# Grouped attention and the norm behind it in one software-pipelined loop

## The chip, the cores and the metric

The kernel runs on one core of a Trainium2 chip. The metric is the device time of one execution in microseconds; of several executions the median is given. The engines are named as in the profile: PE is TensorE (PEld its weight loads), DVE is VectorE, ACT is ScalarE, POOL is GpSimd, SP is the engine that issues most DMAs. Each engine works through its own queue in order and waits on semaphores.

## The reference, cut to what matters

The program is a chain of blocks on a tensor of 16 images with 128 channels and 1024 tokens each, T = 16384 tokens in all. The change touches the last attention block and the norm behind it:

```python
t = t + L3_attn(_ln_t(t), ...)        # grouped attention
t = t + L3_ffn(_ln_t(t), ...)         # routing and experts

# in L3_attn, S = 1024, D = 128, G = 8 groups, H = 4 heads
q = (x @ Wq + bq).reshape(b, s, G, H, d)
k = (x @ Wk + bk).reshape(b, s, G, d)
v = (x @ Wv + bv).reshape(b, s, G, d)
scores = einsum('bqghd,bkgd->bqhg', q, k) / sqrt(d)   # k summed over all its tokens
weights = softmax(scores, axis=-1)                    # over the 8 groups
out = einsum('bqhg,bsgd->bsgd', weights, v).reshape(b, s, G * d)
return out @ Wo + bo

def _ln_t(v):                          # per token, over the 128 channels
    return (v - mean(v)) / sqrt(var(v) + 1e-5)
```

Since the scores use the sum of k over an image's tokens, and the weights enter only as their sum over an image's queries, an image costs little: 1024 x 32 scores from one matrix per image, a softmax over groups of 8, a sum of the weights over tokens and heads (8 numbers), and one 128 x 128 matrix A, the sum over the 8 groups of these numbers times a product of Wv and Wo.

## The kernel before, in words

The residual stream X (128 channels x 16384 tokens) stays in the on-chip memory for the whole program. Blocks follow one another, each with its own queues per engine and a barrier at its end. Three of them matter here; they take the stretch from about 4308 to 4587 us.

`phase_gqa` (from L2103) is grouped attention. It first makes what all images share (products of the weights, the score matrix and score bias of each image), then loops over 16 images b. For each: SP copies the image's normed tokens from Y to one of two buffers `ys` (L2148); PE writes the scores to the one bank `psc` (one product for the bias, L2178, and eight for the tokens, L2181); DVE takes the maximum of each 8 scores (L2251) and writes the differences to the one buffer `sc` (L2254); ACT takes the exponential in place (L2210); DVE sums, inverts and scales (L2260 to L2262, `weights`); PE sums the weights over tokens by a product with ones into the bank `pws` (L2188, `sums`); DVE reduces these to 8 numbers (L2268) and builds A with eight dependent multiply-adds (L2272, `mixing`); PE multiplies A with the image's Y (L2200, `outputs`, two banks `po`); DVE adds the result into X (L2280, `residual`).

The order in each engine's queue is written out by hand. In DVE's step for image b stand: maximum and subtract of b + 1, residual of b - 1, mixing of b, weights of b + 1. The subtract waits for the sums of b, because both use the one buffer `sc`. In PE's step for b stand: scores of b + 2 (after the subtract of b + 1 has emptied `psc`), outputs of b, sums of b + 1. `wait_if` (L383) is a semaphore wait that is left out in the first turns; `over` (L1031) peels the first and last turns of a loop; `Chain` makes each DVE instruction wait for the one before it.

`phase_norm` (L1816) with the tag n4 is the norm behind it, a block of its own over 32 chunks of 512 tokens with four buffers. For each chunk n, by the methods of `LayerNorm` (L1047): SP loads the chunk of X (L1069); PE transposes its four 128 x 128 tiles to token rows (L1076, front); DVE takes statistics (L1090, L1099); POOL makes scale and shift in four small instructions (L1108 to L1114); ACT normalizes (L1123) and issues the store of the token rows to the DRAM tensor `tokens` (L1841); PE transposes back (L1084); DVE copies the result to Y (L1129). Attention and this norm have separate tensors Y (`gqa_Y`, `moe_Y`).

`phase_route` follows, which reads Y, and then the experts, which read `tokens`.

Of the kernel before, what the change touches and what calls it, by code (L numbers as in the profile page):

```python
# [15 lines left out]
AX = mybir.AxisListType  # L16
# [1030 lines left out]
class LayerNorm:  # L1047
# [39 lines left out]
    def vector_stats(self, v, n, u):  # L1087
        v.wait_ge(self.front_ready, n + 1)
        for r in range(4):
            last = v.bn_stats(self.st[u][:, r, :], self.front[u][:, r, :])  # L1090
        last.then_inc(self.stat, 1)


        v.wait_ge(self.stat, 1)
        v.wait_ge(self.stat, n + 1)

        wait_if(v, self.ab_ready, n - self.r + 1)
        for r in range(4):
            last = v.bn_aggr(self.mv[u][:, r, :], self.st[u][:, r, :])  # L1099
        last.then_inc(self.mv_ready, 1)  # L1100
# [1002 lines left out]
def phase_gqa(nc, K, D, X, Y, W, w_in, sums):  # L2103
# [5 lines left out]
    with Mem(nc, "gq") as m:  # L2109
# [10 lines left out]
        sc = m.sb("sc", [C, TL, GH])  # L2120
# [4 lines left out]
        pa = m.ps("pa", [C, CH])  # L2125
        pc = m.ps("pc", [C, CH])
        pv = [m.ps(f"pv{h}", [C, 4, C]) for h in range(2)]
        psc = m.ps("psc", [C, TL, GH])
        pws = m.ps("pws", [C, TL, GH])
# [3 lines left out]
        sw_ready, sb_ready = m.sem("sw_ready"), m.sem("sb_ready")  # L2133
# [3 lines left out]
        NW = 3 + 1 + G8  # L2137
# [3 lines left out]

        with nc.Block() as block:
            @block.sync
            def _(sp):
                def step(b, u, last):
# [4 lines left out]
                over(sp, B, step)  # L2150

            @block.tensor
            def _(pe):
# [7 lines left out]
                last.then_inc(vo_mm, 1)  # L2161
                pe.wait_ge(ks_ready, 1)
# [5 lines left out]
                for g in range(G8):  # L2168
                    last = pe.matmul(pws[:, 0, g:g + 1], wo[:, g, :], bvT[:, g:g + 1], start=True, stop=True)
                last.then_inc(bvo_mm, 1)  # L2170
# [3 lines left out]
                def scores(b, u):  # L2174
                    pe.wait_ge(y_in[u], y_count(b, u))

                    wait_if(pe, sub_ready, b)
                    pe.matmul(psc[:, :, :], K["ident"][:, :], sb_[:, bass.ds(b, 1), :].to_broadcast([C, TL, GH]),  # L2178
                              start=True, stop=False)
                    for t in range(TL):  # L2180
                        last = pe.matmul(psc[:, t, :], ys[u][:, t * C:(t + 1) * C], sw[:, bass.ds(b, 1), :].rearrange("p o g -> p (o g)"),  # L2181
# [3 lines left out]
                def sums(b):  # L2185

                    pe.wait_ge(w_ready, b + 1)
                    pe.matmul(pws[:, :, :], K["ones"][:, :], sc[:, :, :], start=True, stop=True).then_inc(ws_mm, 1)  # L2188

                scores(0, 0)  # L2190
                sums(0)
                scores(1, 1)

                def step(b, u, last):
                    if not isinstance(b, int) or b + 2 < B:
                        scores(b + 2, u)
# [4 lines left out]
                    if not last:  # L2201
                        sums(b + 1)

                over(pe, B, step)

            @block.scalar
            def _(a):
                with a.Fori(0, B) as b:
                    a.wait_ge(sub_ready, b + 1)
                    a.activation(sc[:, :, :], sc[:, :, :], ACT.Exp, scale=C ** -0.5).then_inc(e_ready, 1)  # L2210

            @block.vector
            def _(v):
# [20 lines left out]

                for dst, src, mm, ready in ((sw, pa, sw_mm, sw_ready), (sb_, pc, sb_mm, sb_ready)):
# [5 lines left out]
                v.wait_ge(bvo_mm, 1)  # L2241
                step0(v.tensor_copy(vo[:, :, C], pws[:, 0, 0:G8]))

                scv = sc[:, :, :].rearrange("p t (h g) -> p (t h) g", g=G8)

                pscv = psc[:, :, :].rearrange("p t (h g) -> p (t h) g", g=G8)

                def below_max(b, st):

                    v.wait_ge(s_mm, b + 1)  # L2250
                    st(v.reduce_max(top[:, :], pscv, AX.X))  # L2251

                    wait_if(v, ws_mm, b)
                    v.tensor_tensor(scv, pscv, top[:, :].rearrange("p (t o) -> p t o", o=1).to_broadcast([C, TL * H4, G8]),  # L2254
                                    ALU.subtract).then_inc(sub_ready, 1)

                def weights(b, st):

                    v.wait_ge(e_ready, b + 1)
                    st(v.reduce_sum(red[:, :], scv, AX.X))  # L2260
                    st(v.reciprocal(red[:, :], red[:, :]))
                    v.tensor_tensor(scv, scv, red[:, :].rearrange("p (t o) -> p t o", o=1).to_broadcast([C, TL * H4, G8]),  # L2262
                                    ALU.mult).then_inc(w_ready, 1)

                def mixing(b, u, st):

                    v.wait_ge(ws_mm, b + 1)
                    st(v.reduce_sum(wsum[:, :], pws[:, :, :].rearrange("p t (h g) -> p g (t h)", g=G8), AX.X))  # L2268
# [14 lines left out]
                below_max(0, st)  # L2283
                weights(0, st)
                FIRST = st.n

                def step(b, u, last):
                    st = Chain(v, dstep, NW * b + FIRST)
                    if not last:
                        below_max(b + 1, st)  # L2290
                    if not isinstance(b, int) or b:
                        residual(b - 1, 1 - u)
                    mixing(b, u, st)
                    if not last:
                        weights(b + 1, st)
                        assert st.n == NW

                over(v, B, step)
                residual(B - 1, 1)

# [409 lines left out]
def build(nc, D):  # L2712
    with ExitStack() as ctx:
# [27 lines left out]
        with Mem(nc, "gqa") as m:  # L2741
            Y = m.sb("Y", [C, T])
            sums = m.sb("sums", [C, NCH])
            W, w_in = gqa_weights(m)
            phase_norm(nc, K, X, Y, "n3", sums=sums, early=lambda a: gqa_load(a, D, W, w_in))
            phase_gqa(nc, K, D, X, Y, W, w_in, sums)
        with Mem(nc, "moe") as m:
            Y = m.sb("Y", [C, T])
# [69 lines left out]
```

## Time and profile before

| what | us |
|---|---|
| median of 3 runs | 4887.17 |
| range of the runs | 4884.74 to 4889.07 |
| the profiled execution | 4881.74 |
| its span | 4879.9 |
| PE busy (share of the span) | 4184.0 (86%) |
| DVE busy | 2925.3 (60%) |
| ACT busy | 2181.0 (45%) |
| POOL busy | 1827.4 (37%) |
| mean granted TensorE clock | 0.921 |

The span is the time from the first to the last instruction that the profiler saw; the execution's own time lies 1.8 us above it. Shares are means over stages with different limits: the page's slices show PE at 9 tenths nearly throughout the attention and feed-forward blocks in the middle of the span, and at 5 to 7 tenths, with a lower granted clock, in the last seven slices, where grouped attention, its two norms, the routing and the experts lie. The granted clock has two levels, 1.0 (2.4 GHz) and 0.5 (1.2 GHz); a mean between them is a mixture.

### The profile page before, as it was taken

The numbers are of one execution on the slowest core, as the hardware profiler recorded it, in microseconds if no ns is written. First come the engines' busy times: TensorE is split into PE (matmuls) and PEld (weight loads), VectorE is DVE, ScalarE is ACT, GpSimd is POOL, SyncE is SP. The second block draws the span as 40 slices with busy tenths as digits, with TensorE's granted clock in tenths as the row PEclk, the third lists the DMA queues.
The fourth block names the chain that finished last, engine by engine and source line by source line (L and its number), as shares of the span: only waits on it lengthen the run. The fifth ranks groups of instructions, "written<-read, shape, count | busy, mean of one in ns | idle before, by whom it ended". The sixth has DMA issues, their size and how long they took to land. (4 is left out here: it accounts for less than half of the span.)

```text
span 4879.9 us, 76343 instructions
## 1 busy us (share of the span) xinstructions
PE 4184.0 (86%) x23099; PEld 1656.3 (34%) x23099; DVE 2925.3 (60%) x5621; ACT 2181.0 (45%) x4040; POOL 1827.4 (37%) x1333
## 2 busy tenths in 40 slices
PE   5799999846999999999999999967999999876513
PEld 2343433324222222222222222234444444453312
DVE  4788888656777777777777777742000000256774
ACT  3333333245466656565656566653333333431400
POOL 1100000037477777777777777771000000220401
PEclk9999999979899999999999999988999999966655
DMA  3555645357322222222222222010000000111504
GB/s 138 138 137 118 140 115 136 74 195 253 42 33 33 33 33 33 33 33 33 33 33 33 33 33 33 6 61 29 0 0 0 0 0 0 74 65 47 190 0 151
DMA packets 201952, 313.47 MB, mean 64 GB/s; under 512 B 48887, under 2 KB 132861, under 8 KB 199181
## 3 DMA queue, kind: packets, MB, share of 16 engines
q1 hardware_dynamic: 172296, 270.23, 23.8%
q10 hardware_dynamic: 24960, 28.87, 1.7%
q0 software_dynamic: 4368, 10.07, 0.7%
q8 instruction: 197, 3.23, 0.3%
q14 instruction: 131, 1.07, 0.1%
HBM read 102.88 MB, written 78.12 MB: 37 GB/s over the span
## 5 line engine op out<-in xcount | busy, mean ns | idle before, releaser
L1699 DVE TENSOR_REDUCE at_mx<-at_side 128x1 f32<-128x512 f32 x2048 | 1295.6, 682 | 410.0 <-PE at_side L1600 402.5
L1772 ACT ACTIVATE at_P<-at_S 128x512 f32<-128x512 f32 x2048 | 1115.2, 600 | 702.3 <-PE at_S L1633 692.6
L1532 POOL TENSOR_TENSOR at_pairs<-at_P 128x2048 f32<-128x2048 f32 x256 | 1159.9, 4531 | 238.5 <-ACT at_P L1772 210.7
L1633 PE MATMUL at_S<-at_qo,at_ko 99*128 99x512 bf16 x2048 | 788.2, 387 | 73.3 <-ACT at_P L1772 47.6
L1600 PE MATMUL at_side<-at_ko,at_qo 96*128 96x512 bf16 x2048 | 775.8, 389 | 29.3 <-DMA at_ko<-qk 24.1
L2054 ACT ACTIVATE ff_hs<-ff_ph,ff_b 128x512 f32<-128x512 f32 x512 | 351.7, 687 | 524.4 <-PE ff_ph L2024 524.4
L1644 PE MATMUL at_num<-at_P,at_rvt 128*32 128x512 f32 x4096 | 557.5, 606 | 0.0
L2024 PE MATMUL ff_ph<-ffn_Y,ff_w 128*128 (+1 forms) x1024 | 524.8, 594 | 8.7 <-DMA ff_b<-in_b_dram 8.7
L2038 PE MATMUL ff_po<-ff_hs,ff_w2s 128*128 128x512 f32 x1024 | 522.5, 592 | 0.0
L2073 DVE SCALAR_TENSOR_TENSOR X<-ff_po,ffn_b2w,X 128x512 f32 (+1 forms) x32 | 24.0, 751 | 822.9 <-PE ff_po L2038 822.9
L834 DVE SCALAR_TENSOR_TENSOR la_dwq<-la_pad,la_taps,la_dwq 128x1024 f32<-128x1024 f32 x384 | 491.4, 1280 | 11.1
L1633 PEld LDWEIGHTS at_S<-at_qo,at_ko 99*128 99x128 bf16 x2048 | 198.2, 97 | 879.3 <-ACT at_P L1772 658.0
L1108 POOL TENSOR_TENSOR n_ln_ab<-n_ln_mv,eps 128x4 f32<-128x4 f32 x96 | 19.1, 199 | 1161.0 <-DVE n_ln_mv L1099 1158.3
L582 POOL DMA_DIRECT2D proj<-la_y x32 | 17.4, 544 | 810.3 <-ACT la_y L941 810.3
L619 PE MATMUL la_acc<-la_rep,la_wagg 128*32 128x512 f32 x2560 | 314.6, 609 | 3.8 <-DMA la_rep<-la_pad 3.1
L1600 PEld LDWEIGHTS at_side<-at_ko,at_qo 96*128 96x128 bf16 x2048 | 200.9, 98 | 272.0 <-DVE at_mx L1699 95.0
L2024 PEld LDWEIGHTS ff_ph<-ffn_Y,ff_w 128*128 128x128 f32 x1024 | 195.3, 191 | 254.4 <-issue 245.0
L1655 PE MATMUL at_den<-at_pairs,ones 128*32 128x512 f32 x2048 | 277.3, 614 | 4.5 <-POOL at_pairs L1532 4.4
L2038 PEld LDWEIGHTS ff_po<-ff_hs,ff_w2s 128*128 128x128 f32 x1024 | 194.6, 190 | 245.2 <-issue 244.7
L1123 ACT ACTIVATE n_ln_xt<-n_ln_front,n_ln_ab 128x128 f32<-128x128 f32 x384 | 144.4, 456 | 114.2 <-POOL n_ln_ab L1114 103.8
L1644 PEld LDWEIGHTS at_num<-at_P,at_rvt 128*32 128x32 f32 x4096 | 91.3, 108 | 174.7 <-issue 104.3
L1545 POOL TENSOR_TENSOR at_prod<-at_numT,at_ub 128x1024 f32<-128x1024 f32 x32 | 75.5, 2358 | 185.0 <-DVE at_recT L1728 185.0
(416 smaller groups left out, 4596.4 us busy)
## 6 DMA issues: line engine op xcount, KB each, us to landing
la_rep<-la_pad SPq DMA_DIRECT2D x512, 162.8 KB, 3.6
qk<-ap_part SPq DMA_DIRECT2D x32, 768.0 KB, 3.7
at_qo<-qk SPq DMA_DIRECT2D x384, 64.0 KB, 3.7
at_ko<-qk SPq DMA_DIRECT2D x192, 128.0 KB, 5.8
n_ln_xs<-X SPq DMA_DIRECT2D x96, 256.0 KB, 2.3
u<-ap_us SPq DMA_DIRECT2D x32, 320.0 KB, 4.0
X<-in_x_dram SPq DMA_DIRECT2D x4, 2048.0 KB, 25.6
conv<-conv_Y SPq DMA_DIRECT2D x16, 512.0 KB, 2.6
```

The costliest lines, as they stand in the source:

```text
L619: done = pe.matmul(acc[c][32 * j:32 * j + 32, :], wagg[:, p - 1, j, g, :], view(slice(0, C), p, h, j, *PLACES[g]), start=(c < 2 and g == 0 ...
L834: v.scalar_tensor_tensor(out, image, taps[:, t:t + 1], out, ALU.mult, ALU.add).then_inc(tap_done, 1)
L1532: g.tensor_tensor(pairs[i % 2][:, :, :], P[a][:, :, :], P[a + 1][:, :, :], ALU.add).then_inc(pair_done, 1)
L1600: return pe.matmul(side[bank][:, :], qo[of_u][0:KQ, i // QUAD, s, i % QUAD * C:(i % QUAD + 1) * C], ko[of_u][0:KQ, s, h * CH:(h + 1) * CH] ...
L1633: pe.matmul(S[n % RING][:, :], ko[u][:, h, j * C:(j + 1) * C], qo[u][:, half, h, :], start=True, stop=True).then_inc(s_ready, 1)
L1644: last = pe.matmul(num[32 * i:32 * i + 32, :], rvt[u][:, j, :], P[k % SLOTS][:, i, :], start=(j == 0), stop=(j == 7))
L1655: last = pe.matmul(den[32 * i:32 * i + 32, :], K["ones"][:, 0:32], pairs[(k // 2 - 1) % 2][:, i, :], start=(j == 0), stop=(j == 6))
L1699: v.reduce_max(mx[:, n // 2, n % 2:n % 2 + 1], side[bank][:, :], AX.X).then_inc(side_saved, 1)
L1772: a.activation(P[k % SLOTS][:, i, :], S[(4 * k + i) % RING][:, :], ACT.Exp).then_inc(p_ready, 1)
L2024: pe.matmul(ph[j % R][:, :], w1[:, f, :], Y[:, bass.ds(b * N + half * CH, CH)], start=True, stop=True).then_inc(h_mm, 1)
L2038: done = pe.matmul(po[half][:, :], w2s[u][:, f, :], hs[j % R][:, :], start=(f == 0), stop=(f == FT - 1)).then_inc(h_used, 1)
L2054: a.activation(hs[j % R][:, :], ph[j % R][:, :], ACT.Gelu, bias=b1[:, j % FT:j % FT + 1]).then_inc(h_ready, 1)
```

## The change

`phase_gqa` and the norm n4 become one block, `phase_gqa_norm`, with one Y. In its loop, the step s handles image s and two chunks of the norm behind it. On each engine the queue of a step now holds:

- SP: the load of image s + 3; the loads of chunks 2s - 2 and 2s - 1 from X (each waits for statistics of a chunk before, which stand behind the residual that wrote the chunk); the stores to `tokens` of chunks 2s - 5 and 2s - 4, which ACT issued before.
- PE: front transposes of chunk 2s - 4, back transposes of chunk 2s - 6, scores of s + 2, outputs of s, front transposes of 2s - 3, back transposes of 2s - 5, sums of s + 1.
- ACT: exponential of s + 1; normalization of 2s - 5, copy of the back-transposed chunk 2s - 7 to Y; normalization of 2s - 4, copy of 2s - 6. These copies were DVE's.
- DVE: residual of s - 1, maximum and subtract of s + 1, mixing of s, statistics of 2s - 4, weights of s + 1, statistics of 2s - 3. Mixing stands in front of the statistics.
- POOL: the norm's four small instructions for each chunk, as before.

The loop runs over 16 + 3 or 16 + 4 steps, so the last chunks are drained behind the last image. The norm has two buffers in place of four. `sc` and `psc` become two each; the sums are written into the bank `psc[u]` whose scores have been read, and `pws` goes. So the subtract of b waits for the sums of b - 2 (counted by `ws_mm`, b - 1), and the scores of b + 2 wait for the weight sum of b (`wsum_ready`), not for a subtract. The back transposes take `ln.back` and the bank `pc` in turn; the setup products that had banks of their own use those of the loop. In the setup, the eight products for the value bias (into `pws` before) move from behind the score products to ahead of them, into `psc[1]`, and their copy ahead of the others. The scores of image 1 stand in front of the sums of image 0. In `LayerNorm.vector_stats`, which the other norms use too, the wait for `ab_ready` moves from between the two kinds of statistics to ahead of both.

```diff
     def vector_stats(self, v, n, u):
         v.wait_ge(self.front_ready, n + 1)
+        wait_if(v, self.ab_ready, n - self.r + 1)
         for r in range(4):
             last = v.bn_stats(...)
...
-        wait_if(v, self.ab_ready, n - self.r + 1)
         for r in range(4):
             last = v.bn_aggr(...)
...
+        ln = LayerNorm(m, K, X, 2)
+        pa, pv = ln.back, ln.front
+        back = [ln.back, pc]
+        psc = [m.ps(f"psc{u}", [C, TL, GH]) for u in range(2)]
...
+        def pipeline(eng, step, drain):
+            for s in range(4):
+                step(s, s % 2, False)
+            with eng.Fori(2, B // 2 - 2) as i:
+                for u in range(2):
+                    step(2 * i + u, u, False)
+            for s in range(B - 4, B + drain):
+                step(s, s % 2, s >= B - 1)
...
+                def chunk_in(n, u):                                  # SP
+                    if isinstance(n, int) and n < 2:
+                        sp.wait_ge(x_ready, n + 1)
+                    else:
+                        sp.wait_ge(ln.mv_ready, n - 1)
+                    sp.dma_start(ln.xs[u][:, :], X[:, bass.ds(n * CH, CH)]).then_inc(ln.staged[u], 16)
+                def chunk_out(n, u):
+                    sp.wait_ge(ln.xt_ready, n + 1)
+                    sp.dma_start(tokens[...], ln.xt[u][:, :, :]).then_inc(tok_out[u], 16)
...
                 def scores(b, u):                                    # PE
-                    wait_if(pe, sub_ready, b)
+                    wait_if(pe, wsum_ready, b - 1)
...
+                def channels(n, u):
+                    pe.wait_ge(ln.xt_ready, n + 1)
+                    wait_if(pe, ln.saved, n - 1)
+                    for r in range(4):
+                        last = pe.transpose(back[u][:, r * C:(r + 1) * C], ln.xt[u][:, r, :], K["ident"][:, :])
+                    last.then_inc(ln.back_ready, 1)
+                def step(s, u, last):
+                    if among(2 * s - 4):
+                        ln.tensor_front(pe, 2 * s - 4, 0)
+                    if among(2 * s - 6):
+                        channels(2 * s - 6, 0)
+                    if before(s + 2, B):
+                        scores(s + 2, u)
+                    if before(s, B):
+                        outputs(s, u)
+                    if among(2 * s - 3):
+                        ln.tensor_front(pe, 2 * s - 3, 1)
+                    if among(2 * s - 5):
+                        channels(2 * s - 5, 1)
+                    if before(s + 1, B) and not last:
+                        sums(s + 1, 1 - u)
+                pipeline(pe, step, 3)
...
+                def normal(n, u, save_n):                            # ACT
+                    if among(save_n):
+                        a.wait_ge(ln.back_ready, save_n + 1)
+                    if among(n):
+                        wait_if(a, tok_out[u], 8 * (n - u))
+                        ln.scalar(a, n, u)
+                    if among(save_n):
+                        a.copy(Y[:, bass.ds(save_n * CH, CH)], back[u][:, :]).then_inc(ln.saved, 1)
+                def step(s, u, last):
+                    if before(s + 1, B) and not last:
+                        powers(s + 1, 1 - u)
+                    normal(2 * s - 5, 1, 2 * s - 7)
+                    normal(2 * s - 4, 0, 2 * s - 6)
+                powers(0, 0)
+                pipeline(a, step, 4)
...
-                    wait_if(v, ws_mm, b)                             # DVE, in below_max
+                    wait_if(v, ws_mm, b - 1)
...
+                def step(s, u, last):
+                    if not isinstance(s, int) or s:
+                        residual(s - 1, 1 - u)
+                    st = Chain(v, dstep, NW * s + FIRST)
+                    if before(s + 1, B):
+                        below_max(s + 1, 1 - u, st)
+                    if before(s, B):
+                        mixing(s, u, st)
+                    if among(2 * s - 4):
+                        ln.vector_stats(v, 2 * s - 4, 0)
+                    if before(s + 1, B):
+                        weights(s + 1, 1 - u, st)
+                    if among(2 * s - 3):
+                        ln.vector_stats(v, 2 * s - 3, 1)
+                pipeline(v, step, 1)
+                for n in range(NCH - 2, NCH):
+                    ln.vector_stats(v, n, n % 2)
...
-            phase_norm(nc, K, X, Y, "n4", D["tokens"])
```

## Rows read from the trace of the kernel before

**Rows 1.** Stages: start:end, us, busy of each engine (instructions), granted clock, DMA share, GB/s
```profile
1050.00:1200.00 150.00, 119.67 (x584) 80.20 (x584) 114.42 (x377) 107.76 (x238) 114.21 (x175) 1.00 0.76 275
4250.00:4300.00 50.00, 31.41 (x196) 25.06 (x194) 45.88 (x247) 37.00 (x100) 39.53 (x101) 0.86 0.30 114
4344.00:4500.00 156.00, 104.21 (x343) 61.15 (x344) 99.81 (x248) 24.21 (x29) 0.00 (x0) 0.66 0.11 44
4508.00:4586.00 78.00, 52.96 (x256) 42.15 (x256) 60.68 (x288) 48.11 (x128) 51.05 (x128) 0.68 0.65 209
```

**Rows 2.** One turn of attention's loop in order of time: start, us, engine, line
```profile
4419.89 0.42 DVE L2260 TENSOR_REDUCE gq_red<-gq_sc 128x32 f32<-128x256 f32 x1 [0.15 <-DVE gq_A L2272]
4420.04 3.78 PE L2200 MATMUL gq_po<-gqa_Y,gq_A 128*128 x4 [2.52 <-DVEq L2274]
...
4421.20 0.42 DVE L2251 TENSOR_REDUCE gq_top<-gq_psc 128x32 f32<-128x256 f32 x1
...
4423.61 0.99 PE L2188 MATMUL gq_pws<-gq_sc,ones 128*128 128x256 f32 x2
...
4424.63 0.42 DVE L2254 TENSOR_TENSOR gq_sc<-gq_psc,gq_top 128x256 f32<-128x256 f32 x1 [3.01 <-PE gq_pws L2188]
4424.97 1.40 DVE L2280 SCALAR_TENSOR_TENSOR X<-gq_po,gq_A,X 128x512 f32 x2
...
4425.31 0.69 PE L2178 MATMUL gq_psc<-gq_sbias,ident 128*128 x2 [0.71 <-DVE gq_sc L2254]
...
4425.84 1.87 PE L2181 MATMUL gq_psc<-gq_sw,gq_ys 128*128 x16
4426.29 0.41 DVE L2268 TENSOR_REDUCE gq_wsum<-gq_pws 128x8 f32<-128x256 f32 x1
4426.84 0.35 DVE L2272 SCALAR_TENSOR_TENSOR gq_A<-gq_vo,gq_wsum,gq_base 128x129 f32<-128x129 f32 x1
4427.23 2.69 DVE L2272 SCALAR_TENSOR_TENSOR gq_A<-gq_vo,gq_wsum,gq_A 128x129 f32<-128x129 f32 x7
```

**Rows 3.** First mixing product, last image's seven products, first instruction of the routing
```profile
4344.49 0.35 DVE L2272 SCALAR_TENSOR_TENSOR gq_A<-gq_vo,gq_wsum,gq_base 128x129 f32<-128x129 f32 x1
...
4496.97 2.69 DVE L2272 SCALAR_TENSOR_TENSOR gq_A<-gq_vo,gq_wsum,gq_A 128x129 f32<-128x129 f32 x7
...
4587.35 0.13 POOL L2411 MEMSET sk_gw<- 128x32 f32 x1 [6.94 <-POOLq L57]
```

**Rows 4.** The norm behind attention, in order of time: statistics, normalization, front transposes
```profile
4510.51 0.38 DVE L1099 BATCH_NORM_AGGREGATE n_ln_mv<-n_ln_st 128x2 f32<-128x6 f32 x4
4510.80 0.86 DVE L1090 BATCH_NORM_STATS2 n_ln_st<-n_ln_front 128x6 f32<-128x128 f32 x4
...
4512.06 0.86 DVE L1090 BATCH_NORM_STATS2 n_ln_st<-n_ln_front 128x6 f32<-128x128 f32 x4
...
4512.84 1.50 ACT L1123 ACTIVATE n_ln_xt<-n_ln_front,n_ln_ab 128x128 f32<-128x128 f32 x4 [25.82 <-POOL n_ln_ab L1114]
...
4515.31 1.06 PE L1076 MATMUL n_ln_front<-ident,n_ln_xs 128*128 128x128 f32 x4
...
4520.95 0.60 PE L1076 MATMUL n_ln_front<-ident,n_ln_xs 128*128 128x128 f32 x4
```

**Rows 5.** Groups on ACT from 4305 to 4600: line, tiles, count, busy and mean ns
```profile
L2210 ACT ACT_TABLE_LOAD x16 | 20.5, 1283 | 3.5 <-SPq L57 3.2
L2210 ACT ACTIVATE gq_sc<-gq_sc 128x256 f32<-128x256 f32 x16 | 6.7, 417 | 151.7 <-DVE gq_sc L2254 151.7
L2495 ACT COPY sk_gT<-sk_fr 128x512 f32<-128x512 f32 x5 | 2.9, 585 | 12.4 <-PE sk_fr L2432 12.4
```

**Rows 6.** DMA issues from 4300 to 4600: count, KB each, median us to landing
```profile
n_ln_xs<-X SPq DMA_DIRECT2D x32, 256.0 KB, 2.3
tokens<-n_ln_xt ACTq DMA_DIRECT2D x32, 256.0 KB, 2.5
```

**Rows 7.** The value bias's products and the second image's score products, in order of time
```profile
4327.35 3.41 PE L2169 MATMUL gq_pws<-gqa_bvT,gqa_wo 128*128 128x1 f32 x16
...
4339.75 3.46 PE L2181 MATMUL gq_psc<-gq_sw,gq_ys 128*128 128x32 f32 x16
```

More of the change, by code:

```diff
@@ L2119, in phase_gqa @@
         ys = [m.sb(f"ys{u}", [C, N]) for u in range(2)]
-        sc = m.sb("sc", [C, TL, GH])
+        sc = [m.sb(f"sc{u}", [C, TL, GH]) for u in range(2)]
         red = m.sb("red", [C, TL * H4])
@@ L2144, in _, with images @@
             def _(sp):
[L2145 removed]
+                def images(b, u):
                     wait_if(sp, s_mm, b - 1)
                     sp.dma_start(ys[u][:, :], Y[:, bass.ds(b * N, N)]).then_inc(y_in[u], 16)
[L2150 removed]
+                def chunk_in(n, u):
[6 more added lines that the diff above has]
+                    sp.wait_ge(ln.xt_ready, n + 1)
+                    sp.dma_start(tokens[bass.ds(n * CH, CH), :].rearrange("(r p) c -> p r c", p=C), ln.xt[u][:, :, :])\
+                      .then_inc(tok_out[u], 16)
+                def step(s, u, last):
+                    if before(s + 3, B):
+                        images(s + 3, 1 - u)
+                    if among(2 * s - 2):
+                        chunk_in(2 * s - 2, 0)
+                    if among(2 * s - 5):
+                        chunk_out(2 * s - 5, 1)
+                    if among(2 * s - 1):
+                        chunk_in(2 * s - 1, 1)
+                    if among(2 * s - 4):
+                        chunk_out(2 * s - 4, 0)
+                for b in range(3):
+                    images(b, b % 2)
+                pipeline(sp, step, 3)
+                for u in range(2):
+                    sp.wait_ge(tok_out[u], 16 * NCH // 2)
+            @block.gpsimd
+            def _(g):
+                over(g, NCH, lambda n, u, last: ln.gpsimd(g, n, u))
             @block.tensor
@@ L2161, in _ @@
                 last.then_inc(vo_mm, 1)
+                for g in range(G8):
+                    last = pe.matmul(psc[1][:, 0, g:g + 1], wo[:, g, :], bvT[:, g:g + 1], start=True, stop=True)
+                last.then_inc(bvo_mm, 1)
                 pe.wait_ge(ks_ready, 1)
@@ L2282, in _, with step @@
                 st = Chain(v, dstep)
-                below_max(0, st)
-                weights(0, st)
+                below_max(0, 0, st)
+                weights(0, 0, st)
                 FIRST = st.n
[L2287 to L2295, printed above, removed]
-                        assert st.n == NW
-                over(v, B, step)
-                residual(B - 1, 1)
+                def step(s, u, last):
+                    if not isinstance(s, int) or s:
[5 more added lines that the diff above has]
+                        mixing(s, u, st)
+                    if among(2 * s - 4):
+                        ln.vector_stats(v, 2 * s - 4, 0)
+                    if before(s + 1, B):
+                        weights(s + 1, 1 - u, st)
+                        assert st.n == NW
+                    if among(2 * s - 3):
[3 more added lines that the diff above has]
+                    ln.vector_stats(v, n, n % 2)
 E8 = 8
```

76 lines of the change are left out of this document (35 added, 41 removed).

## The prediction

> **What bounds the kernel now.** The page's chain of waits holds only the experts' scatter and gather at the very end, so it says nothing of the change; the stretch that the change touches has to be read by stage. I take it from the first mixing product of grouped attention (4344.49) to the first instruction of the routing (4587.35): 242.9 us, 5.0% of the span [rows 3]. The table by stage shows no full engine in it: in attention's loop VectorE is busy 99.8 of 156 us and TensorE 104.2 at a granted clock of 0.66; in the norm's loop VectorE 60.7 of 78 and TensorE 53.0 at 0.68 [rows 1]. So waits make the time, and one turn of attention's loop shows them [rows 2]: mixing ends, 0.30 us later TensorE starts the outputs (3.57 us until the sums), the sums take 0.99, and only then does VectorE get on (subtract at 4424.63, after 3.01 us of waiting), through residual, weight sum and eight products to 4429.92. That is 4.6 us of TensorE and 5.3 of VectorE in series, 10.2 with the hops. Over the loop the period is (4496.58 - 4344.49) / 15 = 10.14 us, where 4496.58 is the start of the last image's first product, 0.39 before its other seven [rows 2, 3]. After the last product (4499.66) 87.7 us pass until the routing, nearly all of it the norm [rows 3].
>
> **The change, part by part.** The norm's 32 chunks move into attention's loop, two a step, four to six chunks behind the image. The sum is then one of three parts: 2 steps without norm work, 13 with it, and a tail.
>
> VectorE's work in a step, from start to start in rows 2: weights 1.31 (4419.89 to 4421.20), maximum 0.46 (0.42 and a gap), subtract 0.34, residual 1.32, weight sum 0.55, products 3.08 and 0.15 after them: 7.21. Two chunks' statistics add 2 x 1.26 (4510.80 to 4512.06) [rows 4]: 9.73 us. The copy of the transposed chunk goes to ScalarE.
>
> The chain through TensorE that must fit beside it: end of the products, 0.30, outputs, the odd chunk's four transposes, its statistics 1.26, residual 1.32, maximum and subtract 0.80, weight sum 0.55, products 3.08. The outputs take 3.57 us in rows 2, where the clock stands at its lower level, 1.2 GHz; at 2.4 GHz I estimate half, 1.78. The transposes are seen at both levels: 0.60 and 1.06 [rows 4]. So the step is 9.7 at full clock and 11.9 at half: with a hop or two 9.8 and 12.0. The subtract no longer waits for the sums of the same turn, since it writes the other buffer; what is late next is the odd chunk's statistics, which stand behind the outputs in TensorE's queue, and with them residual and everything after on VectorE.
>
> The second loop, through GpSimd and ScalarE, closes over two steps: even statistics, 1.95 until ScalarE starts (4510.89 to 4512.84), normalize 1.50, front and back transposes 1.2, scores 2.4 (4425.31 to 4427.71), outputs 1.8, odd transposes 0.6, then 1.26 + 1.32 + 0.80 + 0.55 + 3.08 + 1.26: 17.7 at full clock, 8.9 a step, so it hides behind 9.8; at half some 23, again near 12 [rows 2, 4].
>
> TensorE's work in a step at full clock: scores 2.4, outputs 1.78, sums 0.5, sixteen transposes some 2.4: 7.1, or 72% of 9.8. At half, with 3.46 for the scores' 16 passes [rows 7] and 1.2 for the bias: 4.7 + 3.57 + 0.99 + 4.2 = 13.5, and then TensorE is the bound. The clock decides between these. By rows 1 the stage that keeps TensorE 80% busy at full clock is granted 1.00, the norm before attention 0.86 at 63% busy, attention 0.66 and this norm 0.68. By rows 2 the scores run at full clock after 4.6 us of unbroken work, and the outputs at half after 2.5 us of idleness. Counted from the end of the products, the new step at full clock runs: outputs 0.3 to 2.1, odd transposes to 3.3, sums to 3.8; idle until ScalarE is done with the even chunk at 4.8 (1.26 + 1.95 + 1.50); transposes to 6.0; scores from the weight sum's end at 6.6 to 9.0; the next outputs at 10.1. So the gap ahead of the outputs falls to about 1 us, and none is longer than about 1.1. I take the step mostly at full clock, one in five at half: 9.8 + 0.2 x 2.2 = 10.2.
>
> ScalarE: exp 0.42, eight normalizations 3.0, two copies of 0.585 [rows 4, 5]: 4.6 of 10.2, hidden; the copy stands in front of nothing but the next normalization, which has 2 us to spare. The table load that follows each exp in the loop (16 of 1.28 us [rows 5]) should go, since the first exp now stands ahead of the loop; were it to stay, ScalarE would have 5.9 of 10.2 and still not bind. SP: each step issues the image's load and two loads and two stores of a chunk. The load of chunk 2s-2 waits for statistics, lands after 2.3 us [rows 6] and is wanted 4 us after issue; the stores (2.5) have a whole step. Behind each waiting DMA on SP stand only the next loads; covered as long as landing stays under 4 us; each us above that costs 13. GpSimd does what it did. The wait on ab_ready that moves ahead of the statistics is always met there, because the save of the chunk before it has passed: 0 in the other norms too. The added semaphore on the weight sum replaces a step of the same chain: 0.
>
> Ahead of the loop the bias products (3.41 us [rows 7]) come before the two products whose copies release the scores, where they ran beside the copies: between 0 and +3.4, about 1.8 by the overlap that is lost. Against it, the second image's scores now run during the first softmax instead of after its sums; that gives back at most their 3.46 and 1.2, and the sums wait for them. I take 0 for both together, between -3 and +3.
>
> Tail, from the last product: outputs, odd front and statistics 27 until about 5; residual 6.5; then chunks 28 to 31, each pair waiting for normalization of the pair before: statistics 28 at 8, GpSimd and normalize 11.5, front 30 and statistics 13.5, and 1.5 to 2.5 later the odd one, 15.5; GpSimd, normalize, back transposes and copy 1.95 + 1.5 + 1.1 + 0.6 = 20.7; the last store lands 2.5 after normalize, 21.5. With TensorE at half in so thin a stretch I take 24, bounds 20 and 29, and 1.4 for the barrier: 25.4, in place of 87.7.
>
> The sum: 2 steps at 10.14 (no norm work yet) and 13 at 10.2 make 152.9, in place of 152.1: +0.8. The tail: -62.3. Together -61.5, from the profiled execution's 4881.74: 4820.2. That execution lay 5.4 below the median of the runs (4887.17, from 4884.74 to 4889.07), so I put the median after at **4826**. Each 0.1 us of the step moves it by 1.3.
>
> **Rivals.**
> (a) TensorE stays at half clock in the outputs and transposes: step 12.0, 23.4 more, 4849. For it: every output of the loop before runs at half [rows 2], and 72% busy is below the 80% of the one stage granted 1.00 [rows 1]. Against: the idle gap ahead of the outputs shrinks from 2.5 to 1 us. [...]
> (b) TensorE at half for all its work: it is the bound at 13.5 and the overlap is mostly handed over, so the change gives little of what it is built for: 3.3 x 13 = 43 more, 4869. Against: work without a gap is what preceded full clock in rows 2.
> (c) A load or ScalarE is late by about 1 us a step, because 1.5 MB a step now share the DMA queues: step 11.2, 4839. For: chunk loads have only 1.7 us of slack. Against: the norm's own stage moved 209 GB/s and still landed loads in 2.3 us [rows 1, 6].
> (d) Slower: the front transposes at the head of TensorE's step wait for load, statistics, GpSimd and normalize of the chunk whose buffer they reuse, and hold scores and outputs behind them, so that one chunk's chain, 2.3 + 1.06 + 1.26 + 1.95 + 1.5 + 1.1 = 9.2, lies in series with attention's 10.14. Step 19.3, 118 more, 4944. It decides from a step of 14.9, where 4.7 of the 9.2 are uncovered. Against: the chunk is four to six behind the image and its chain has a step to run in.
>
> **How the numbers follow.** Forecast, with steps of 9.7 to 11 (4815 to 4837): 0.60. (a) 0.18, (c) 0.09, (b) 0.08, (d) 0.05. The range: from 4811 (step 9.7, tail 20, a start 3 us earlier) to 4862, which takes in (a) and (c) with a late tail, and leaves out (b) and (d) and a little. A measurement can tell about 0.2%, 10 us, from none. Faster by over that: all of the forecast, (a), (c) and nearly all of (b) (it stays 18 below): 0.92. Within: a step between 14 and 15.6, 0.03. Slower: 0.05.
>
> **What would show it.** Right: no separate norm stage between attention's last product and the routing, some 25 us there; VectorE over 90% busy in the loop with a period near 10.2; granted clock 0.85 or more; no wait of the subtract for the sums; ScalarE without table loads in the loop; waits on VectorE mainly for the odd chunk's front. Wrong in the clock: a granted clock near 0.67 and VectorE waiting 2 us a step for front or sums. Wrong in the overlap: TensorE waiting over 4 us a step at the front transposes for ScalarE or for a load. The forecast fails if the step is over 11.5 us or the tail over 40.

## The result and the profile after

| what | before | after |
|---|---|---|
| median of 4 runs each (us) | 4885.95 | 4846.81 |
| range of the runs | 4883.24 to 4889.07 | 4842.97 to 4850.70 |
| the profiled execution, its span | 4881.74, 4879.9 | 4842.97, 4841.3 |
| PE, DVE, ACT busy (us) | 4184.0, 2925.3, 2181.0 | 4168.8, 2903.1, 2176.6 |
| mean granted TensorE clock | 0.921 | 0.924 |

The ratio is 0.992, with a 95% interval from 0.9903 to 0.9937: faster by 39 us. The forecast was 4826; the time lies 21 us above it, inside the range, and 2 us from the price of rival (a).

The stages of the changed kernel, the loop and the tail (columns as in [rows 1]):

```profile
4373.00:4520.00 147.00, 110.50 (x475) 77.38 (x473) 109.98 (x397) 52.28 (x135) 40.63 (x102) 0.76 0.37 125
4523.00:4548.00 25.00, 14.07 (x52) 9.53 (x51) 8.61 (x50) 12.97 (x32) 9.64 (x24) 0.57 0.37 116
```

VectorE is busy 75% of the loop, not over 90%, and the granted clock is 0.76: neither half nor full. The ends of the stretch, which answer [rows 3], in order of time:

```profile
4349.80 0.35 DVE L2360 SCALAR_TENSOR_TENSOR gq_A<-gq_vo,gq_wsum,gq_base 128x129 f32<-128x129 f32 x1
...
4519.48 0.35 DVE L2360 SCALAR_TENSOR_TENSOR gq_A<-gq_vo,gq_wsum,gq_base 128x129 f32<-128x129 f32 x1
4519.86 2.69 DVE L2360 SCALAR_TENSOR_TENSOR gq_A<-gq_vo,gq_wsum,gq_A 128x129 f32<-128x129 f32 x7
...
4548.60 0.13 POOL L2502 MEMSET sk_gw<- 128x32 f32 x1 [5.48 <-POOLq L57]
```

The period is (4519.48 - 4349.80) / 15 = 11.31 us, where it was 10.14; the tail is 26.05, where it was 87.7. From the first mixing product to the routing 198.8 us pass in place of 242.9. One turn, VectorE and TensorE, which answers [rows 2]:

```profile
4450.68 0.35 DVE L2360 SCALAR_TENSOR_TENSOR gq_A<-gq_vo,gq_wsum,gq_base 128x129 f32<-128x129 f32 x1
4450.79 0.69 PE L2227 MATMUL gq_psc<-gq_sbias,ident 128*128 x2 [1.99 <-DVE gq_wsum L2355]
...
4451.32 2.32 PE L2230 MATMUL gq_psc<-gq_sw,gq_ys 128*128 x16
...
4454.06 3.78 PE L2247 MATMUL gq_po<-late_Y,gq_A 128*128 x4 [0.42 <-DVEq L2362]
4454.08 0.89 DVE L1092 BATCH_NORM_STATS2 gq_ln_st<-gq_ln_front 128x6 f32<-128x128 f32 x4 [0.32 <-DVE gq_A L2360]
...
4457.63 1.06 PE L1076 MATMUL gq_ln_front<-ident,gq_ln_xs 128*128 128x128 f32 x4
...
4458.81 0.89 DVE L1092 BATCH_NORM_STATS2 gq_ln_st<-gq_ln_front 128x6 f32<-128x128 f32 x4 [2.20 <-PE gq_ln_front L1076]
...
4462.65 0.41 DVE L2355 TENSOR_REDUCE gq_wsum<-gq_psc 128x8 f32<-128x256 f32 x1
...
4463.20 0.69 PE L2227 MATMUL gq_psc<-gq_sbias,ident 128*128 x2 [2.37 <-DVE gq_wsum L2355]
```

The scores run at or near full clock, the outputs behind them at half (3.78, estimated 1.78 at full). The odd chunk's front stands behind the outputs in TensorE's queue, so its statistics wait 2.20 us on VectorE; with them come late the residual, the weight sum, and the next scores, for which TensorE stands idle 2.37. That is the gap that the forecast had at 1 us or less. What VectorE waits for over the loop, and then TensorE (us in total, times, longest):

```profile
DVE gq_ln_st L1092 <- PE gq_ln_front L1076: 24.7, 13, 3.2
DVE gq_ln_st L1092 <- DVE gq_A L2360: 3.4, 12, 0.3
```
```profile
PE gq_psc L2227 <- DVE gq_wsum L2355: 22.2, 11, 2.5
PE gq_po L2247 <- DVEq L2362: 10.9, 10, 4.4
```

On ScalarE the table loads of [rows 5] are gone but for the first, and the copies cost what was estimated (0.585):

```profile
L2289 ACT COPY late_Y<-gq_ln_back 128x512 f32<-128x512 f32 (+1 forms) x16 | 9.6, 597 | 0.0
...
L2279 ACT ACT_TABLE_LOAD x1 | 1.3, 1283 | 3.4 <-PEq L57 3.4
```

### The profile page after: what moved, and what is told of

Read it like the earlier page. It is cut to its first block and busy times, and to the rows that moved or that the text cites. A ratio compares the mean times of both kernels' runs of the same rounds, so it can differ in the third digit from the quotient of the medians.

```text
span 4841.3 us, 76196 instructions
## 1 busy us (share of the span) xinstructions
PE 4168.8 (86%) x23099; PEld 1654.4 (34%) x23099; DVE 2903.1 (60%) x5589; ACT 2176.6 (45%) x4057; POOL 1829.5 (38%) x1333
## 5 line engine op out<-in xcount | busy, mean ns | idle before, releaser
L1123 ACT ACTIVATE n_ln_xt<-n_ln_front,n_ln_ab 128x128 f32<-128x128 f32 x256 | 96.4, 456 | 69.5 <-POOL n_ln_ab L1114 67.7
```

## The experiments

Theory after the result: the clock. TensorE's outputs at half make the front late, VectorE waits 1.9 us a turn, and the gap that follows ahead of the scores brings the clock down again. Rivals: queue order alone, the loads, or a price of the parts that the clock has no share in. Below, a turn is the time from one image's first mixing product to the next one's, and "step" stands for the mean of all 15 turns of the profiled execution, the two without norm work among them. Clock and busy times are those of 4373 to 4500 where no other stretch is named, and each ratio is to the kernel before in the same job. An idle product is a matrix product that nobody reads.

**One part alone: the wait.** The kernel before, with only the wait of `vector_stats` moved.

```diff
         v.wait_ge(self.front_ready, n + 1)
+        wait_if(v, self.ab_ready, n - self.r + 1)
...
-        wait_if(v, self.ab_ready, n - self.r + 1)
```

> The kernel before with one edit of the change: the wait for ab_ready moves ahead of the statistics, in all the norms. In the profile after the change, the two norms ahead of grouped attention were each 2.8 us longer. Theory: the moved wait is met when it is reached and that length is chance, so no difference (within 3 us of before). Rival: the moved wait costs, 5 to 9 us over three or four norms, ratio 1.001 to 1.002.

4888.43 against 4884.70, ratio 1.0007 [0.9998, 1.0016]. No cost of it is shown; by the interval up to 8 us isn't excluded either, so the rival's 5 to 9 is not wholly ruled out.

**Keep TensorE in work.** The changed kernel with idle products (128x512) ahead of scores and outputs; they land in a bank that is overwritten.

```diff
+                def fill(s, k):
+                    wait_if(pe, x_ready, 2 * s - 1)
+                    for _ in range(k):
+                        pe.matmul(po[0][:, :], K["ident"][:, :], Y[:, bass.ds(s * N, CH)], start=True, stop=True)
...
                     if before(s + 2, B):
+                        fill(s, 2)
                         scores(s + 2, u)
                     if before(s, B):
+                        fill(s, 1)
                         outputs(s, u)
```

> The changed kernel with idle gaps of TensorE filled: two 128x512 float32 products ahead of the scores and one ahead of the outputs, into the bank po0 which the outputs then overwrite (nothing reads them). Theory, clock: the outputs run at half clock because TensorE idles ahead of them; with the gaps filled they and the odd chunk's transposes run at full clock, VectorE's wait of 2.0 us for them goes, and the loop's step falls from 11.3 to about 10, total about 4830 (ratio 0.988). Rival, queue order: the wait is a matter of the order alone, the outputs stay at half or the fillers delay the scores as much as they save: step 11.3 to 12.5, total 4847 to 4865.

4823.44, ratio 0.9877 [0.9862, 0.9892]; the step is 10.0. More work for TensorE made the loop 20 us shorter. The stage:

```profile
4373.00:4500.00 127.00, 107.25 (x539) 70.80 (x540) 108.98 (x391) 52.27 (x136) 39.64 (x99) 0.99 0.43 145
```

**Which gap.** Two idle products ahead of the scores only.

```diff
+                        fill(s, 2)
                         scores(s + 2, u)
```

> The changed kernel with only the two fillers ahead of the scores (two 128x512 float32 products into po0, which nothing reads). In the profile after the change TensorE idles 2.0 us ahead of the scores and 0.4 to 1.0 ahead of the outputs. Theory: the longer gap is what puts the clock down by the time of the outputs, so this alone brings them to full clock and the step to about 10: ratio 0.988. Rival: the short gap ahead of the outputs matters too, outputs stay half in most steps: step 11 or more, ratio 0.991 or above.

4825.47, ratio 0.9867 [0.985, 0.9883]; step 9.97. The stage:

```profile
4373.00:4500.00 127.00, 102.89 (x525) 69.53 (x524) 110.40 (x398) 50.71 (x131) 38.65 (x96) 0.96 0.41 139
```

One ahead of the outputs only:

```diff
+                        fill(s, 1)
                         outputs(s, u)
```

> The changed kernel with only the one filler ahead of the outputs. Theory: the gap of 2.0 us ahead of the scores stays and with it half clock in most outputs; the filler itself then takes up to 1.7 us at half clock and delays the outputs by up to 1: step 11.3 to 12.5, ratio 0.992 to 0.995. Rival: filling the last gap ahead of the outputs is what counts, step about 10, ratio 0.988.

4850.33, ratio 0.992 [0.9903, 0.9936]; step 11.28: nothing gained. So of these two gaps the one ahead of the scores is the one that counts. But this loop, in its profiled execution, ran in two ways one after the other. Its two stretches, and TensorE on either side of the change, with VectorE's wait in the first long turn:

```profile
4380.00:4440.00 60.00, 47.31 (x248) 32.43 (x248) 52.79 (x192) 22.39 (x59) 19.23 (x48) 0.97 0.41 142
4440.00:4520.00 80.00, 63.41 (x256) 42.31 (x256) 57.02 (x205) 27.87 (x72) 19.22 (x48) 0.76 0.34 114
```
```profile
4430.32 0.69 PE L2227 MATMUL gq_psc<-gq_sbias,ident 128*128 x2 [0.41 <-DVE gq_wsum L2361]
...
4433.49 1.90 PE L2247 MATMUL gq_po<-late_Y,gq_A 128*128 x4
...
4438.58 0.66 PE L1076 MATMUL gq_ln_front<-ident,gq_ln_xs 128*128 128x128 f32 x4 [1.69 <-ACT gq_ln_xt L1123]
4439.08 0.97 PE L2259 MATMUL gq_ln_back<-ident,gq_ln_xt 128*128 128x128 f32 x4
4440.45 1.22 PE L2227 MATMUL gq_psc<-gq_sbias,ident 128*128 x2 [0.41 <-DVE gq_wsum L2361]
4441.46 3.46 PE L2230 MATMUL gq_psc<-gq_sw,gq_ys 128*128 x16
...
4446.58 3.32 PE L2247 MATMUL gq_po<-late_Y,gq_A 128*128 x4
...
4450.47 0.89 DVE L1092 BATCH_NORM_STATS2 gq_ln_st<-gq_ln_front 128x6 f32<-128x128 f32 x4 [4.09 <-PE gq_ln_front L1076]
...
4454.55 0.69 PE L2227 MATMUL gq_psc<-gq_sbias,ident 128*128 x2 [2.46 <-DVE gq_wsum L2361]
...
4459.07 3.62 PE L2247 MATMUL gq_po<-late_Y,gq_A 128*128 x4
```

With the outputs at full clock six turns take 9.7 to 10.6, and in the last four of them the gap ahead of the scores is 0.4 to 0.8 us; with the outputs at half the turns take 11 to 14, and the gap is 1.9 to 2.8 in most of them. The order of events at the change tells which came first. The clock fell ahead of the gap: the back transposes at 4439.08 take 0.97 in place of 0.65 and the scores 3.46 in place of 1.87, behind a wait of 1.69 for ScalarE and a gap of 0.41, both of which the turn at full clock before it had too. Only then is the front late (VectorE waits 4.09), and the long gap of 2.46 comes a turn later. So here the gap is the clock's effect, where the idle products ahead of the scores showed it as its cause; what started the fall in this turn the rows don't tell.

**Can the good turns keep themselves up?** Idle products in both places, in steps 0 to 7 alone.

```diff
+                        if isinstance(s, int) and s < 8:
+                            fill(s, 2)
...
-                pipeline(pe, step, 3)
+                pipeline(pe, step, 3, 8)
```

> The changed kernel with two idle products ahead of the scores and one ahead of the outputs in steps 0 to 7 alone (TensorE's queue writes eight steps out in place of four); steps 8 to 15 are those of the changed kernel. My theory: the loop has two states that keep themselves up. With the outputs at full clock VectorE doesn't wait for the odd chunk's front, the weight sum comes early and the gap ahead of the scores stays near 0.4 to 0.8 us, as in the first five turns of the kernel with one idle product ahead of the outputs; with the outputs at half VectorE waits 2 us, the gap grows to 2.4 and the clock falls again. So at least some of the steps 8 to 15 go on at about 10 us after the last idle product; if all eight do, about 4825 and a ratio of 0.988. Rival: the gap that is left without the products lowers the clock by itself; then the turns are long again at once, eight of 11.8 in place of 10: 14 us more, about 4838, ratio 0.9905.

4838.34, ratio 0.9895 [0.9878, 0.9911]: the rival's number. The last turn with idle products took 12.91, and those behind it 12.05, 12.53, 11.39, 11.97, 11.18, 11.69 and 10.90:

```profile
4429.90 1.88 PE L2247 MATMUL gq_po<-late_Y,gq_A 128*128 128x512 f32 x4
4436.73 0.98 PE L2227 MATMUL gq_psc<-gq_sbias,ident 128*128 x2 [2.78 <-DVE gq_wsum L2364]
...
4440.78 3.47 PE L2247 MATMUL gq_po<-late_Y,gq_A 128*128 x4
```

The long turns came at once and stayed. The entry was no clean one, though: the last two idle products ahead of scores had themselves come to half clock (3.54, where 1.88 is usual), behind a wait of 1.77 for ScalarE, and the first gap without them was already 2.78. That long turns keep themselves up is seen here; that short ones do without help is not, and in the loop with one idle product the short ones ended with no longer gap ahead of the scores. Whether they could from a clean entry stays open.

**Take VectorE's wait off the outputs.** The changed kernel with the odd chunk's front ahead of the outputs in TensorE's queue.

```diff
-                    if before(s, B):
-                        outputs(s, u)
                     if among(2 * s - 3):
                         ln.tensor_front(pe, 2 * s - 3, 1)
+                    if before(s, B):
+                        outputs(s, u)
```

> The changed kernel with one swap in TensorE's queue: the front transposes of the odd chunk stand ahead of the outputs (they wait only for ScalarE's normalization, which is done some 2 us before). Theory, queue order: VectorE's wait for the odd chunk goes whatever the clock is, since weights and both statistics (3.8 us) then lie beside the outputs at half clock (3.9 with the hop): step from 11.3 to about 10, total about 4830 (ratio 0.988), with the outputs still at half clock. Rival: the transposes delay the outputs by their 1.06 and the residual waits instead: step 11 to 11.5, total 4842 to 4850.

4824.19, ratio 0.9879 [0.9864, 0.9894]; step 9.73, with no idle product. The stage, a turn with outputs at half and the outputs behind it, and the first waits of VectorE and TensorE:

```profile
4373.00:4500.00 127.00, 98.49 (x478) 70.62 (x479) 112.12 (x406) 54.19 (x140) 40.76 (x103) 0.87 0.43 147
```
```profile
4414.96 0.77 PE L1076 MATMUL gq_ln_front<-ident,gq_ln_xs 128*128 128x128 f32 x4 [1.69 <-ACT gq_ln_xt L1123]
...
4417.52 3.46 PE L2230 MATMUL gq_psc<-gq_sw,gq_ys 128*128 x16
4420.79 1.09 PE L1076 MATMUL gq_ln_front<-ident,gq_ln_xs 128*128 128x128 f32 x4
...
4421.68 3.62 PE L2247 MATMUL gq_po<-late_Y,gq_A 128*128 x4
...
4422.25 0.89 DVE L1092 BATCH_NORM_STATS2 gq_ln_st<-gq_ln_front 128x6 f32<-128x128 f32 x4
...
4427.47 0.69 PE L2227 MATMUL gq_psc<-gq_sbias,ident 128*128 x2 [0.21 <-DVE gq_wsum L2355]
...
4430.85 1.98 PE L2247 MATMUL gq_po<-late_Y,gq_A 128*128 x4 [0.51 <-DVEq L2362]
```
```profile
DVE gq_ln_st L1092 <- DVE gq_A L2360: 3.6, 13, 0.3
DVE X L2368 <- PE gq_po L2247: 2.0, 3, 1.0
```
```profile
PE gq_ln_front L1076 <- ACT gq_ln_xt L1123: 21.3, 13, 2.1
```

Outputs at half still occur (3.62) but no longer hold up the statistics; VectorE's wait for the front is gone, and the scores come 0.2 us after what went before. So the clock still falls, but a fall doesn't last: the next outputs are at full clock again (1.98). TensorE's idle time now lies ahead of the even front (21.3 us in 13 waits for ScalarE, 1.6 each), the falls come behind it, as in the two loops above, and the clock is 0.87. Whether that wait is what starts them was not tried. The idle products reached the same time in the old order, so order alone isn't the cause, and the loop that moves 125 GB/s after moves 147 here, so the loads were not the limit.

**The parts of the change alone.** First, the attention loop with its two banks, and the norm behind it as a block of its own.

```diff
-        sc = m.sb("sc", [C, TL, GH])
+        sc = [m.sb(f"sc{u}", [C, TL, GH]) for u in range(2)]
...
-                    wait_if(pe, sub_ready, b)
+                    wait_if(pe, wsum_ready, b - 1)
```

> The changed kernel's attention loop with two score banks and the new order, but without the norm in it; the norm runs behind it as a block of its own, as before. Theory: two banks alone take the sums out of the chain, and the step falls from 10.14 to 9.0 at half clock (products 3.1, outputs 3.6, residual, maximum, subtract and weight sum 2.4), so 4869 to 4870 (ratio 0.9965); the rest of the gain is the norm. Rival: the whole gain of attention comes from the overlap with the norm, and without it the step stays at 10.1: 4884 (ratio 0.9995). Second rival: the gap ahead of the outputs shrinks enough for full clock, and the step falls to 7.5: 4846 (ratio 0.992).

4880.39 against 4884.70, ratio 0.9991 [0.9982, 1.0]. The first four turns take 9.67, 7.13, 8.12 and 8.80, the next eight 9.3 to 10.3: mean 9.40. By groups of one line (count, busy us, mean ns, idle ahead):

```profile
L2241 PE MATMUL gq_po<-late_Y,gq_A 128*128 (+1 forms) x52 | 47.8, 1074 | 10.2 <-DVEq L2356 10.1
L2224 PE MATMUL gq_psc<-gq_sw,gq_ys 128*128 (+1 forms) x176 | 33.8, 363 | 0.0
...
L2221 PE MATMUL gq_psc<-gq_sbias,ident 128*128 (+1 forms) x22 | 11.2, 605 | 15.2 <-DVE gq_wsum L2349 15.2
```

Most outputs are at half as before, and now the scores too in many turns: 33.8 us for 11 images are 3.1 each, where [rows 2] have 1.87 and [rows 7] 3.46. With idle products, one ahead of the scores and one ahead of the outputs:

```diff
                     if before(s + 2, B):
+                        fill(s, 1)
                         scores(s + 2, u)
                     if before(s, B):
+                        fill(s, 1)
                         outputs(s, u)
```

> The attention loop with two banks and no norm in it (norm behind, a block of its own), and one idle product ahead of the scores and one ahead of the outputs in every step; the products land in a bank that is overwritten. My theory: in that kernel the second bank shortened the first four steps to 7.1 to 8.1 us and the half clock gave it back in the rest (10.2); with TensorE kept in work the step stays near 8, 15 x 1.4 = 21 us less than with 9.4, ratio about 0.994. Rival: the long steps have another cause than the clock; the step stays at 9.4 or grows by the added products (0.4 us), ratio 0.999 to 1.001.

4850.20, ratio 0.9927 [0.991, 0.9943]; step 7.72, and the tail as before (90.4 against 90.8, from the last image's first product). From 4373 to 4450, where this loop ends sooner:

```profile
4373.00:4450.00 77.00, 68.32 (x279) 40.08 (x278) 65.18 (x159) 4.16 (x10) 0.00 (x0) 0.93 0.15 62
```

So the second bank, with the order that comes with it, is worth 15 x 2.4 = 36 us near full clock, and the clock took most of it back.

Second, the order: the even chunk's statistics ahead of mixing in VectorE's step.

```diff
-                    if before(s, B):
-                        mixing(s, u, st)
                     if among(2 * s - 4):
                         ln.vector_stats(v, 2 * s - 4, 0)
+                    if before(s, B):
+                        mixing(s, u, st)
```

> The changed kernel with one part undone: on VectorE the statistics of the even chunk stand ahead of mixing, not behind it. Theory, chain through TensorE: the 1.26 us of statistics no longer lie beside the outputs but in the chain from residual to the products, so VectorE waits 1.3 longer for the odd chunk and the step grows from 11.3 to 12.5: 4864 (ratio 0.9955). Rival, VectorE's total work sets the step: the order is of no matter, ratio 0.992.

4870.31, ratio 0.9961 [0.9947, 0.9975]; step 13.1. Mixing ahead of the statistics is worth 0.4%. What VectorE waits for is again the odd front:

```profile
DVE gq_ln_st L1092 <- PE gq_ln_front L1076: 33.5, 10, 4.5
```

Third, the copies: back on VectorE, in the kernel with the front first.

```diff
...
-                        a.copy(Y[:, bass.ds(save_n * CH, CH)], back[u][:, :]).then_inc(ln.saved, 1)
...
+                            v.tensor_copy(Y[:, bass.ds(n * CH, CH)], back[w][:, :]).then_inc(ln.saved, 1)
```

> The loop with the odd chunk's front ahead of the outputs, and the copies of the chunks' sums back on VectorE (two a step, 0.69 us each in the norm of the kernel before). My theory: with the front ahead of the outputs a step is VectorE's own work (9.73 us), so the copies are paid in full: step 9.73 + 2 x 0.69 = 11.1, 16 x 1.38 = 22 us more than that kernel (4824), about 4846, ratio to the kernel before 0.992. Rival: VectorE still has slack in a step that TensorE sets; then the step stays at 9.7 to 10 and the ratio at 0.988.

4835.93, ratio 0.989 [0.9873, 0.9906]: between the two numbers. The fifth to the eleventh turn take 11.01 to 11.03 each, as the theory had it, but its starting point was wrong: with the front first the turns in the middle take 10.2 on average (9.81 where the outputs are at full clock, up to 11.06 where not), not 9.73, a mean that holds the short second turn of 7.13, without the norm. By these two profiles the copies cost 0.8 a turn, 12 us. The medians show less: the ratios, 0.989 and 0.9879, are 5 us apart and their intervals overlap, and the profiled execution was the slowest of its four here (4844.94) and the fastest there (4817.98). So that the copies belong on ScalarE is not shown by the time.

**The kernel before once more**, for where its attention begins.

> The kernel before, unchanged, profiled once more, for the time at which grouped attention begins: 4307.7 us in the first profile, and 4313.0 to 4315.2 in the five profiles of kernels with the moved wait. Theory: the 5 to 7 us are chance of the profiled execution, so this one may begin anywhere from 4307 to 4315. Rival: the moved wait costs them, and this one begins near 4308 again.

4889.76. Its first mixing product stands at 4352.42, 7.9 us later than in [rows 3], in the same kernel; the loop (151.9) and the tail (87.7) are the same.

**A step further.** The kernel with the front first, and the multiplication by the inverse sums (L2349, `gq_sc` by `gq_red`) on GpSimd. The expectation calls it the norm's by mistake.

```diff
+                    wait_if(v, w_ready, b)
...
-                    v.tensor_tensor(scv[u], scv[u], red[...], ALU.mult).then_inc(w_ready, 1)
+                    v.sem_inc(r_ready, 1)
...
+                def multiply(b, u):                                  # POOL
+                    g.wait_ge(r_ready, b + 1)
+                    x = sc[u][...]
+                    g.tensor_tensor(x, x, red[...], ALU.mult).then_inc(w_ready, 1)
```

> The loop with the odd chunk's front ahead of the outputs, and the multiplication of the norm's result by its weights (0.47 us of VectorE a step) given to GpSimd. My theory: a step there is VectorE's own work (9.73 us), so it falls to about 9.3, 16 x 0.47 = 7.5 us less than 4824, about 4817, ratio 0.9865. Rival: what follows waits for GpSimd, which takes longer for the same multiplication (about 1 us as its other operations of that size take); then no gain, 0.988, or up to 0.5 us a step more, 0.9895.

4817.37, ratio 0.9856 [0.9839, 0.9872]; step 9.57. GpSimd takes 0.63 us, not 1 (the operation of the norm that takes it 1.01 is one of 128x4, not of this size), and the sums wait for it 1.4 us a turn:

```profile
PE gq_psc L2253 <- POOL gq_sc L2203: 15.0, 11, 1.6
```

It has the lowest time of all, but its interval overlaps that of the kernel with the front first, and the two were not run in one job: that it is the better one isn't shown.

## Why the prediction was right in sign and range, and 21 us off

By its own terms, from the profiled executions:

| term | forecast | measured | error |
|---|---|---|---|
| attention's begin (work upstream) | 0 | +7.2 | +7.2 |
| begin (first sum over tokens) to the first product | 0 (±3) | 34.9 - 36.75 = -1.85 | -1.85 |
| two steps without norm | 20.28 | 9.67 + 7.12 = 16.79 | -3.5 |
| thirteen steps with it | 132.6 (10.2 each) | 152.89 (11.76 each) | +20.3 |
| tail | 25.4 | 26.05 | +0.65 |

The errors add up to +22.8, and 4820.2 + 22.8 = 4843.0 is the time of that execution. Of the 7.2 nothing need belong to the change: a second execution of the kernel before begins as late. So the 2 us between the measured time and the price of rival (a) are in part luck: the late begin hides that the loop and the stretch ahead of it were 8.5 us shorter than (a) has them.

**Right.** The norm's stage is gone and the tail is what was worked out (26.05 for 25.4); in it TensorE is at 0.57 of its clock, as assumed. The bias products ahead of the loop cost nothing, the table loads went, the subtract no longer waits for the sums, no load was late (TensorE's waits in the loop show none, and 2.1 us in all for ScalarE), and no cost of the wait in `vector_stats` was seen. What is late next was named: the odd chunk's statistics behind the outputs.

**Wrong: "I take the step mostly at full clock, one in five at half".** This is the mis-sized term: 10.2 was forecast, 11.76 measured. In the profile after, the outputs of step 1 run at full clock (1.98); from step 3 on nearly all take 3.25 to 3.78:

```profile
4362.66 1.98 PE L2247 MATMUL gq_po<-late_Y,gq_A 128*128 128x512 f32 x4 [0.71 <-DVEq L2362]
...
4381.84 3.76 PE L2247 MATMUL gq_po<-late_Y,gq_A 128*128 128x512 f32 x4
```

At 12.0 for such a step, as the forecast had it, 11.76 is nine in ten at half. That is rival (a), which had a chance of 0.18, and the step is over the 11.5 that the prediction itself named as the forecast's failure. The total lies inside the range only because the range took in (a).

The step that failed is the sketch under it, "none is longer than about 1.1". The gaps were worked out from a turn that was already at full clock. In such turns of the loop with one idle product the gap ahead of the scores is about right, 0.4 to 0.8, but the one ahead of the even chunk's transposes, put at 1.0, is 1.69, and the clock fell behind it. And a turn with outputs at half makes its own gap, since they hold back the front, VectorE's statistics and all behind them: 2.0 to 2.4. The forecast watched the gap ahead of the outputs; that one did shrink, from 2.5 to between 0.4 and 1.0, and the outputs stayed at half. The forecast had both steps of this chain, the late front and the clock that follows gaps, and didn't close them into a ring; it asked whether the good turn is consistent, and not whether the bad one is too. The experiments cut the ring in two places, and either cut gives back what was missing: idle products in the gap (4823 to 4825) or a front that doesn't stand behind the outputs (4824). These are the forecast's 4826, and the thirteen turns with norm work take 9.9 to 10.25, where it had 10.2.

The Trainium skill (TensorE: Matmul & The Clock Gate, A second HAM failure mode: psum-queue depth-cycling) says that short idle spells between groups of matmuls, with the banks taken in turn, can be enough to make the clock go back and forth. The trace agrees: the clock is 0.76 here with gaps of 2.0 to 2.4 us ahead of the scores, and 0.99 with idle products ahead of scores and outputs.

**Too high: the first two steps.** Without norm work the loop is the one with two banks: 7.12 in the second step, not the 10.14 of before. The forecast gave the second bank no gain there.

**Not asked: what the second bank does without the norm.** It takes the sums off VectorE's chain and breaks TensorE's work at the same time. Before, the scores ran at full clock 0.7 us behind outputs and sums [rows 2]; with two banks they wait 1.4 us for the weight sum, and the clock falls to 0.59. With idle products the same loop is at 0.93 and its turn at 7.72. So the clock is why the banks alone gave nothing that can be told from no change.

## What to carry to other kernels

Where one engine's clock depends on its gaps, work out the turn twice, once at each level, and ask of both whether the gaps that come out keep that level up. Here the slow turn kept itself up and the fast one was not seen to. A chain gets free of it by its order: what another engine waits for stands ahead of long work that nobody waits for soon. The clock may still fall then, but the fall doesn't feed itself. Where the order can't be changed, try work that does nothing, in the longest gap.

## What the runs showed of the hardware

Two idle products of 128x512 ahead of the scores in each turn made the turn 1.34 us shorter (11.31 to 9.97). The gap ahead of the scores doesn't slow the scores in the turn shown of the changed kernel (2.32 us, near the 1.87 of full clock) but the outputs that follow them (3.78): an instruction that runs slow need not stand next to the gap that slows it. And the time ahead of the changed stretch moves by itself: the first mixing product of all these kernels stands between 4344 and 4363 us, so a term of a few microseconds is read from its own stretch, not from the totals.
